# Rows kept for the last sum: from a copy in SBUF to a scatter into HBM and a gather back; norms by a two-tensor instruction

## The reference, cut to what matters

```
xn   = layernorm(x) * ln_w + ln_b
u    = xn @ Ws.T + bs + xn @ Wi.T + bi
h_t  = tanh(h_{t-1} @ A.T + u_t)                    # 256 steps, 32 sequences side by side
attn = (h @ Wo.T + bo) * sigmoid(xn @ Wg.T + bg) + x
x1   = norm(x + attn)                               # norm: (v - mean) / sqrt(var + eps)
scores = softmax(x1 @ gate_w.T);  the 2 best of scores + gate_b are taken, weighted by scores
expert(v) = silu((v @ w1 + b1) * (v @ w3 + b3)) @ w2 + b2     # hidden width 176
y    = sum over the 8 experts of weight * expert(x1), and the shared expert(x1)
out  = norm(x1 + y)
```

## Time and profile before

| what | value |
|---|---|
| time, median of 3 runs | 724.96 us (724.84 to 725.49) |
| profiled execution: span from first to last instruction | 721.4 us |
| what lies around the span (median less span; the page gives no time of its own for the profiled execution) | 3.6 us |
| instructions | 11625 |
| busy: PE, DVE, ACT, POOL | 679.6, 526.7, 482.4, 438.7 us |
| DMA | 11.28 MB, mean 16 GB/s |
| granted clock of PE | 0.997 of full, mean |

### The profile page before, as it was taken

How to read it: one execution, slowest core, us unless ns; L and a number is a source line. 1 busy time by engine, 2 the same in 40 slices (tenths; PEclk the granted TensorE clock), 3 DMA queues, 4 the chain that set the end, 5 groups by cost and what they waited for, 6 DMA issues and landing times. The chain is left out here.

```text
span 721.4 us, 11625 instructions
## 1 busy us (share of the span) xinstructions
PE 679.6 (94%) x3063; PEld 446.4 (62%) x3063; DVE 526.7 (73%) x1580; ACT 482.4 (67%) x978; POOL 438.7 (61%) x389
## 2 busy tenths in 40 slices
PE   4689999999999999999999999999999999999894
PEld 1255666666666666666666666666666666668672
DVE  6658587776868777686876869677686867678763
ACT  2347676677767676776767667676766767677773
POOL 5145757556584755758466575746657575576753
PEclk9999999999999999999999999999999999999998
DMA  5000000000000000000000000000000000000000
GB/s 171 15 1 16 0 15 16 15 1 15 16 15 15 15 15 0 15 15 15 15 1 20 8 15 15 15 15 0 15 15 15 15 15 2 1 15 2 15 1 30
DMA packets 9425, 11.28 MB, mean 16 GB/s; under 512 B 1198, under 2 KB 5300, under 8 KB 9396
## 3 DMA queue, kind: packets, MB, share of 16 engines
q1 hardware_dynamic: 8346, 10.23, 4.5%
q10 hardware_dynamic: 1050, 0.72, 0.3%
HBM read 6.75 MB, written 4.19 MB: 15 GB/s over the span
## 5 line engine op out<-in xcount | busy, mean ns | idle before, releaser
L308 POOL TENSOR_TENSOR low<-full,high 128x512 fp32r<-128x512 f32 x176 | 226.8, 1289 | 194.1 <-ACT high L392 192.7
L628 DVE SCALAR_TENSOR_TENSOR zt<-p,bcol,t 128x512 f32<-128x512 f32 (+1 forms) x208 | 155.1, 746 | 155.2 <-ACT t L403 137.8
L403 ACT ACTIVATE t<-p,bcol 128x512 f32<-128x512 f32 x192 | 132.1, 688 | 130.0 <-PE p L757 129.8
L613 DVE TENSOR_TENSOR full<-prw,sl 128x512 f32<-128x512 f32 x176 | 119.6, 680 | 7.7 <-issue 3.4
L347 ACT ACTIVATE hT<-pu,bu 16x32 f32<-16x32 f32 x256 | 78.2, 305 | 66.0 <-PE pu L714 66.0
L382 ACT ACTIVATE sl<-zt 128x512 f32<-128x512 f32 x176 | 109.1, 620 | 0.4
L322 POOL TENSOR_TENSOR ex_ex<-napier,ex_ls 128x8 f32<-128x8 f32 x64 | 106.6, 1674 | 4.0 <-DVE ex_ls L520 4.0
L392 ACT ACTIVATE high<-full 128x512 fp32r<-128x512 f32 x176 | 108.5, 616 | 0.7 <-DVE full L613 0.7
L755 PE MATMUL p<-x1h,w1l 128*128 128x512 f32 (+1 forms) x208 | 98.9, 475 | 0.1
L714 PEld LDWEIGHTS pu<-hT,aT 128*16 128x16 f32 x512 | 28.9, 96 | 99.9 <-issue 85.6
L755 PE MATMUL p<-x1h,w3l 128*128 128x512 f32 x192 | 87.1, 454 | 0.0
(11 more groups left out here) (150 smaller groups left out, 1087.1 us busy)
## 6 DMA issues: line engine op xcount, KB each, us to landing
xt<-in_L_attn_x SPq DMA_DIRECT2D x16, 256.0 KB, 3.1
out<-yo SPq DMA_DIRECT2D x16, 256.0 KB, 2.5
w3f<-in_L_ffn_w ACTq DMA_DIRECT2D x1, 704.0 KB, 4.8
w1f<-in_L_ffn_w SPq DMA_DIRECT2D x1, 704.0 KB, 4.9
w2t<-in_L_ffn_w SPq DMA_DIRECT2D x1, 704.0 KB
w1f<-in_L_ffn_sw SPq DMA_DIRECT2D x1, 88.0 KB, 4.6
wg_t<-in_L_attn_Wg SPq DMA_DIRECT2D x1, 64.0 KB, 2.3
w3f<-in_L_ffn_sw SPq DMA_DIRECT2D x1, 64.0 KB, 4.2
```

Source lines behind the costliest of these rows:

```text
L308: g.tensor_tensor(out=lo[0:R, :], in0=full_of(pos)[0:R, :], in1=hi[0:R, :].bitcast(fp32), op=ALU.subtract).then_inc(low_ready, 1)
L403: nc.scalar.activation(t3[(par + pos) % 2][:, :], p3[(par + pos) % 2][:, :], ACT.Identity, bias=b3c[:, pos:pos + 1]).then_inc(t3_ready, 1)
L613: nc.vector.tensor_tensor(out=full_of(pos)[:, :], in0=prw[:, :], in1=sl[pos % 2][:, :], op=ALU.mult).then_inc(s_ready, 1)
L628: nc.vector.scalar_tensor_tensor(out=zt[(par + pos) % 2][0:R, :], in0=p1[(par + pos) % 2][0:R, :], scalar=b1c[0:R, pos:pos + 1], in1=t3[(p ...
```

## The change

Three things are changed.

The copy of the normed x1 into `x1kept` on DVE (slot 28) is gone. In its place POOL issues, in every pass with `attn` (k from -1 to 14), four indirect scatters of 128 rows of 512 B from x1 to `xrows`, a tensor of 1024 rows in HBM: two after the `low` of position 6 and two after that of position 7; and four indirect gathers of the same rows from `xrows` into `x1kept`, two after the `low` of position 11 and two after that of position 12. The row numbers come from `rows_at`, written once by an iota. Ahead of each pair stands a small addition (128x4) into a spare buffer, which carries the waits.

Waits are added: POOL's scatter on `x1_ready`, its gather on all scatters of the tile and on the last sum that read the buffer (`v2_ready`); DVE's first sum on the scatters of the tile before; DVE's last sum on the gathers. `xrows` is filled once with 1024 rows of the input, by a DMA from HBM to HBM which SP issues second, ahead of the small weights.

`normalize` uses a scalar-tensor-tensor instruction in place of a tensor-scalar one: the mean stays a pointer to one value a partition, 1/deviation becomes a second tensor operand, broadcast along the 128 features.

```
--- before.py
+++ after.py
@@ -32,7 +32,7 @@
     AT_START = dict(ho=1, xnT=2, gate=6, u=3, chain=4, ogT=4, x1T=12, x1l=14, logits=15, router=16,
                     second_xnT=9, second_gate=14)
 
-    AT_POOL = dict(mid=3, fresh=5, out=8, exp=9)
+    AT_POOL = dict(mid=3, fresh=5, out=8, exp=9, scatter=6, gather=11)
     NAPIER = 2.718281828459045
 
 
@@ -99,6 +99,10 @@
         yT = sb("yT", [D, TOK])
         yo = sb("yo", [P, Q, D])
 
+        rows_at = [sb(f"rows_at{i}", [P, Q], mybir.dt.int32) for i in range(2)]
+        xrows = nc.dram_tensor("xrows", (2 * TOK, D), fp32).ap()
+        spare = [[sb(f"spare{i}_{j}", [P, Q]) for j in range(8)] for i in range(2)]
+
         stats = {w: sb(f"stats_{w}", [P, Q, 6]) for w in ("in", "mid", "out")}
         mv = {w: sb(f"mv_{w}", [P, Q, 2]) for w in ("in", "mid", "out")}
         ve = {w: sb(f"ve_{w}", [P, Q]) for w in ("in", "mid", "out")}
@@ -126,6 +130,7 @@
         expert_weights_ready, sel_ready = sem("expert_weights_ready"), sem("sel_ready")
         x_loaded = [sem("x_loaded0"), sem("x_loaded1")]
         out_stored = sem("out_stored")
+        rows_scattered, rows_gathered, rows_known, rows_filled = sem("rows_scattered"), sem("rows_gathered"), sem("rows_known"), sem("rows_filled")
         bn_done = {w: sem(f"bn_done_{w}") for w in ("in", "mid", "out")}
         mv_ready = {w: sem(f"mv_ready_{w}") for w in ("in", "mid", "out")}
         pool_r = {w: sem(f"pool_r_{w}") for w in ("in", "mid", "out")}
@@ -224,6 +229,7 @@
                 return v.rearrange("(a d) -> a d", a=1)
 
             sp.dma_start(xt[0][:, :, :].rearrange("p q d -> p (q d)"), xv[0]).then_inc(x_loaded[0], 16)
+            sp.dma_start(xrows, x[0:2 * TOK // S].rearrange("b s d -> (b s) d")).then_inc(rows_filled, 16)
             for dst, src in ((ws_t, Ws), (wi_t, Wi), (a_t, A), (wg_t, Wg)):
                 sp.dma_start(dst[:, :], src).then_inc(state_weights_loaded, 16)
             sp.dma_start(xt[1][:, :, :].rearrange("p q d -> p (q d)"), xv[1]).then_inc(x_loaded[1], 16)
@@ -267,6 +273,8 @@
             g.wait_ge(pool_step, 1)
             g.affine_select(out=ident[:, :], in_=ident[:, :], compare_op=ALU.not_equal, fill=1.0,
                             base=0, pattern=[[-1, P]], channel_multiplier=1).then_inc(id_made, 1)
+            for i in range(2):
+                g.iota(rows_at[i][:, :], pattern=[[P, Q]], base=i * TOK, channel_multiplier=1).then_inc(rows_known, 1)
             g.memset(neghalf[:, :], -0.5)
             g.memset(eps1[:, :], EPS)
             g.memset(eps4[:, :], 4 * EPS)
@@ -325,6 +333,23 @@
                         low_part(pos - 2, k)
                     elif fin and pos < 2:
                         low_part(POS - 2 + pos, k - 1)
+                    if AT_POOL['scatter'] <= pos < AT_POOL['scatter'] + 2 and attn:
+                        g.wait_ge(x1_ready, k + 2)
+                        g.wait_ge(rows_known, 2)
+                        g.wait_ge(rows_filled, 16)
+                        g.tensor_tensor(out=spare[par][pos - AT_POOL["scatter"]][:, :], in0=neghalf[:, :], in1=neghalf[:, :], op=ALU.add)
+                        for q in range(2 * (pos - AT_POOL['scatter']), 2 * (pos - AT_POOL['scatter']) + 2):
+                            g.indirect_dma_start(out=xrows[:, :], out_offset=bass.IndirectOffsetOnAxis(ap=rows_at[1 - par][:, q:q + 1], axis=0),
+                                                 in_=x1[:, q, :], in_offset=None).then_inc(rows_scattered, 16)
+                    if AT_POOL['gather'] <= pos < AT_POOL['gather'] + 2 and attn:
+                        g.wait_ge(rows_scattered, 16 * Q * (k + 2))
+                        if fin:
+                            g.wait_ge(v2_ready, k)
+                        g.tensor_tensor(out=spare[par][pos - AT_POOL["scatter"]][:, :], in0=neghalf[:, :], in1=neghalf[:, :], op=ALU.add)
+                        for q in range(2 * (pos - AT_POOL['gather']), 2 * (pos - AT_POOL['gather']) + 2):
+                            g.indirect_dma_start(out=x1kept[1 - par][:, q, :], out_offset=None, in_=xrows[:, :],
+                                                 in_offset=bass.IndirectOffsetOnAxis(ap=rows_at[1 - par][:, q:q + 1], axis=0),
+                                                 ).then_inc(rows_gathered, 16)
                 if isinstance(k, int) and k == -2:
                     selector()
             iterations(g, one)
@@ -493,8 +518,9 @@
             def normalize(w, src, dst, tile, ready):
                 v.wait_ge(pool_r[w], 2 * tile + 2)
                 for q in range(Q):
-                    ins = nc.vector.tensor_scalar(out=dst[:, q, :], in0=src[:, q, :], scalar1=mv[w][:, q, 0:1],
-                                                  scalar2=rstd[w][:, q:q + 1], op0=ALU.subtract, op1=ALU.mult)
+                    ins = nc.vector.scalar_tensor_tensor(out=dst[:, q, :], in0=src[:, q, :], scalar=mv[w][:, q, 0:1],
+                                                         in1=rstd[w][:, q:q + 1].to_broadcast([P, D]),
+                                                         op0=ALU.subtract, op1=ALU.mult)
                 ins.then_inc(ready, 1)
 
             def bc(t):
@@ -569,6 +595,7 @@
                                                    op0=ALU.add, op1=ALU.mult).then_inc(og_ready, 1)
                 if slot == AT['x1'] and attn:
                     v.wait_ge(ogT_ps, k + 2)
+                    wait(v, rows_scattered, 16 * Q * (k + 1))
 
                     nc.vector.scalar_tensor_tensor(out=x1[:, :, :], in0=xt[1 - par][:, :, :], scalar=4.0,
                                                    in1=out_bank(k)[:, :].rearrange("p (q d) -> p q d", q=Q),
@@ -585,15 +612,13 @@
                     router(slot - at('router', k), k + 1)
                 if slot == AT['v2'] and fin:
                     v.wait_ge(y_ps, k)
+                    v.wait_ge(rows_gathered, 16 * Q * k)
                     wait(v, out_stored, 16 * (k - 1))
                     nc.vector.tensor_tensor(out=yo[:, :, :], in0=pm[:, :].rearrange("p (q d) -> p q d", q=Q),
                                             in1=x1kept[1 - par][:, :, :], op=ALU.add).then_inc(v2_ready, 1)
                 if slot == AT['moments_out'] and fin:
                     v.wait_ge(v2_ready, k)
                     moments("out", yo, k - 1)
-                if slot == AT['kept'] and attn:
-                    v.wait_ge(x1_ready, k + 2)
-                    nc.vector.tensor_copy(x1kept[1 - par][:, :, :], x1[:, :, :])
                 if slot == AT['moments_in'] and pre:
                     v.wait_ge(x_loaded[1 - par], 16 * (half + 2 + par))
                     moments("in", xt[1 - par], k + 3)
```

22 lines of the change are left out of this document (19 added, 3 removed).

## The result

| what | before | after |
|---|---|---|
| time, median | 725.23 us (724.84 to 725.59, 4 runs) | 809.97 us (809.36 to 811.14, 4 runs) |
| ratio, with its 95% interval | | 1.1176 [1.1157, 1.1194] |
| profiled execution: span | 721.4 us | 807.6 us |
| granted clock of PE, mean | 0.997 | 0.938 |

The span grew by 86.2 us; the forecast was 740, with a range up to 785. Where the time went is read in the order in which the forecast was made. First the page after, busy times: us, share, instructions.

What follows compares the result with a forecast made beforehand. PE was taken to bound the kernel; steady tiles 9.8, start 4.4, fill 0.5 and norms and copy 0 gave 14.7 us on the profiled 721.4, a span near 736, with 3.6 for the median 739.7, said as 740; range 724 to 785.

Steps and rivals of the forecast that it cites:

- the collision: DVE's `ex_rw` against a POOL low part: rt and x late 0.1 us without it, 1.2 with; 0.65 taken per tile.
- Faster: Rival: moved low part clears `ex_rw`, rt and x come earlier, PE uses its 0.69 us idle; 717 us, chance 0.10.
- The sum: Whole kernel: 9.8 + 4.4 + 0.5 + 0 = 14.7 us added to the profiled 721.4.
- multiplied by 15: Steady loop: 0.65 us a tile over 15 tiles (passes 0 to 14), 9.8 us, bounds 1.5 and 18.
- one issue: POOL held 1.29 us by each indirect DMA; a pair with its small addition 2.8 us.
- `row_sum` was to wait: DVE's row sum in each steady tile waits about 2.4 us for the late fourth exponential.
- The start: Pass -1: scatters delay the exponentials 1.6 us, a gather pair adds 2.8; 4.4 us lost once.
- the fill: Filling `xrows` ahead of the small weights at the start: between 0 and 2 us, taken as 0.5.
- The norms and the missing copy: On DVE: two-tensor norms -0.1 to +0.1 us each, taken as 0; dropping the copy worth 0.
- The gathers' data: Waits on gathers cost nothing: they end a whole pass before DVE's last sum wants them.
- low parts hold PE nowhere: Sign: low parts should still never hold PE; 3.9 us of delay fits within 5.9 us of play.
- Dear: Rival: an indirect DMA issue takes 1.5 us or more; at 1.67, 767 to 778 us; chance 0.28.

Runs made afterwards that it cites:

- run 4: Kernel after, plus a GpSimd wait for rt ahead of the first low part of a pass: 737.71 us, ratio 1.0169.
- run 9: Kernel after, plus a GpSimd wait for rt ahead of the second low part of a pass, not the first: 747.93 us, ratio 1.0314.
- run 5: Kernel after, plus 12 more PE matmuls per tile just ahead of its wait for rt: 787.81 us, ratio 1.0869.
- run 1: Kernel before with only the two-tensor norms; no scatter or gather, copy kept: 725.54 us, ratio 1.0003.
- run 6: Kernel before, plus a GpSimd wait for rt ahead of the second low part of a pass: 712.84 us, ratio 0.9823.
- run 10: Kernel after with all four gathers in a row behind the last low part of position 12, behind the fourth exponential: 799.31 us, ratio 1.1027.
- run 3: Kernel before, copy and old norms kept, with additions and 128x1450 memsets on POOL at the places of the scatters and gathers: 793.51 us, ratio 1.0939.
- run 12: As run 3, but the last pair of memsets is 128x1820 in place of 128x1450: 812.16 us, ratio 1.1196.
- run 14: As run 3, but the pair ahead of the three low parts is a 128x700 memset and one real gather: 806.97 us, ratio 1.1124.
- run 2: Kernel after with the old tensor-scalar norms; scatters, gathers and their waits kept: 809.21 us, ratio 1.1165.

## Why the prediction was wrong, step by step

**The step that failed** is the collision: "if DVE meets the following low part instead, by 1.2", from which 0.65 us a tile was taken, 9.8 in all. DVE did meet low parts, and by the forecast's own times nearly so: it put `ex_rw` 0.15 us ahead of the end of the gathers, and it came 0.15 us behind the start of the low parts. But the price was set as if there were one low part. POOL, late by the scatters and gathers, has three waiting, and they run as one block of 3.7 us. The forecast's own times had the beginning of it: the low part behind the gathers was to end at 351.4, when the next one (350.70 before) was already due, and its rival "Faster" says that two follow without a gap. No price was put on that. Measured: 3.63 us for `ex_rw`, 3.17 us more from PE's transposes of `og` to those of `rt` (386.93 less 380.53 after, 350.80 less 347.57 before). Runs 4 and 9 show it: the same work on POOL with a pause gives 737.7 and 747.9.

**A term that was missing** is PE's clock. The sum took a stop of PE at its length. In the steady tiles, behind 3.0 us of standing still, the granted clock was 0.52 to 0.62 for about 7 us; run 5 gives this as 2.0 us a tile, so 3.2 us of stop cost 5.2. Over the 14 periods the two are 70.0 us, where the forecast had 9.8 for 15.

**Pass 14 isn't like the others.** The forecast multiplied by 15. In pass 14 the recurrence has ended and PE has less to do, so that POOL with 10.8 us more work becomes what is waited for: the exponential is 5.0 us late for DVE. Of the 10.6 us lost behind the last x, 8.6 are still there in run 4, where no collision is left. No run takes these 8.6 us apart further.

**Right:** one issue was taken as 1.29 us, and it is 1.31 to 1.34 from start to start (a pair with its addition 2.7, taken as 2.8). `row_sum` was to wait 2.4 us and waits 1.93. The start was to lose 4.4 by POOL and 0.5 by the fill, and lost 4.3 and 1.25. The norms and the missing copy were put at 0, and run 1 gives 1.0003 for the norms; the copy alone has no run. The gathers' data are never waited for: they land after 2.5 us. That low parts hold PE nowhere is right for the steady tiles (PE waits for them 4.5 us in all, at the end).

**The rivals.** "Dear" gave 767 to 778 by an issue of 1.67 us, which is not what happened; its ingredient, DVE late and PE standing 2 to 3 us for `rt`, is, at the price of 1.3 us per issue. "Faster" rested on the collision going away if `ex_rw` is clear of the low parts. That is what run 6 does in the kernel before, 12 us faster. The Trainium skill, "SBUF — State Buffer", Who interferes with whom, was cited for `ex_rw` to pass beside the gathers' descriptors. In the kernel after, `ex_sc` does so (0.18 us, at 380.27, within the issue that began at 380.19), but in run 10 `ex_rw`, coming 0.49 us into the last issue ahead of the low parts, doesn't (4.28 us). With another gather behind the issue it does in the same run (0.19 us, at 752.78). So the trace agrees for the issue itself, and `ex_rw` was shut out only where the low parts stood behind it.

## What to carry to other kernels

When work is added to an engine that others collide with, don't price the collision as one of its instructions: look what will be queued up behind the delay, for a block without a pause can hold a short vector instruction for all of its length (3.6 us here). Put a wait that makes GpSimd let the short instruction on the critical path go first; here two lines were worth 72 of 85 us in the kernel after, and 12 us in the kernel before. And price a stop of the matrix engine with what follows it, not by its length alone: here 3.2 us of stop cost 5.2.

## What the runs showed of the hardware that was not expected

- A run of GpSimd instructions without a pause kept a DVE instruction with two SBUF inputs out for the whole run, 3.6 us over three low parts, in the steady tiles with an indirect DMA just ahead of it; with memsets ahead, DVE got in at each boundary (0.55, 1.30, 1.18 us for three instructions in a row). One tile of run 3 was held for the whole run without any DMA (4.32 us), so this is no rule. Memsets of 0.55 us in the run did not let it in (4.57 us).
- A DVE copy of 8 elements was held too, by a memset until its end (0.82 and 1.44 us in runs 3 and 12, 0.17 free) and by the run behind an indirect DMA (3.94 us in run 14). The Trainium skill, "SBUF — State Buffer", Who interferes with whom, says that only the port pair that DVE shares with GpSimd causes contention, as an exclusive lock held for a whole instruction. The single collisions (1.29 us) agree; the holds over three and more instructions go beyond one.
- Alone, the two-tensor norm is hardly slower: the first four took 1.14 us in run 1, against 1.11 us. At the second norm of the start it is faster, as it is not held there. GpSimd begins a memset of 128x1408 at that moment. The four tensor-scalars took 4.16 us in the kernel before and in run 2, to the end of that memset and of two instructions behind it; the four two-tensor ones took 1.14 us in the kernel after and in run 1. Run 1 has no gain in the whole time from it. The row of the kernel before, then that of the kernel after:

```profile
11.51 4.16 DVE L496 TENSOR_SCALAR xn<-xt,mv_in,rstd_in 128x128 f32<-128x128 f32 x4 [1.48 <-POOL rstd_in L301]
```

```profile
12.77 1.14 DVE L521 SCALAR_TENSOR_TENSOR xn<-xt,mv_in,rstd_in 128x128 f32<-128x128 f32 x4 [1.47 <-POOL rstd_in L309]
```
